# A four-block transformer layer for 16 sequences: which weights are prepared ahead of the step table

## The reference

```python
x = x + attn_a(layernorm(x), Wq, bq, Wk, bk, Wv, bv, Wo, bo)   # 16 heads, window of 32 either side, 4 global tokens, softmax
x = x + ffn(layernorm(x), w_gate, w_up, w_down)                # hidden 768, int32 weights / 127, silu(gate) * up
x = x + attn_b(layernorm(x), Wqkv, Wout, bout)                 # rotary, causal, denominator from scores without rotation
x = x + ffn(layernorm(x), w_gate, w_up, w_down)                # the same weights again
```

## Time and profile before

| | us |
|---|---|
| median of three runs | 2028.87 (2023.63 to 2030.54) |
| the profiled execution | 2020.54 |
| its span, first to last instruction | 2018.3 |
| TensorE busy | 1802.5 (89%) |
| VectorE busy | 1429.3 (71%) |
| ScalarE busy | 1429.0 (71%) |
| GpSimd busy | 803.8 (40%) |
| mean granted TensorE clock | 0.946 |

### The profile page before, as it was taken

The page is one execution under the profiler, slowest core; times in us unless marked ns, Lnnn a source line. Parts: engine busy times, 40 slices in busy tenths (PEclk is TensorE's granted clock), DMA queues, the critical chain, the costliest instruction groups (busy, mean ns, idle before and its releaser), DMA issues.

```text
span 2018.3 us, 63373 instructions
## 1 busy us (share of the span) xinstructions
PE 1802.5 (89%) x25221; PEld 1140.4 (57%) x25221; DVE 1429.3 (71%) x2978; ACT 1429.0 (71%) x3591; POOL 803.8 (40%) x1140
## 2 busy tenths in 40 slices
PE   5577999999899999999899999999999999998775
PEld 3363556566565655656565565656565565655444
DVE  6374768677686867768786877778786777865634
ACT  2227787786868778786877869686877868687590
POOL 0423343533434343443434344343435434344431
PEclk9687999999998999999999999999999999999897
DMA  5223344352524435253534525253443525243321
GB/s 155 64 56 90 87 129 98 100 119 77 136 63 131 91 101 124 78 130 69 137 78 116 122 76 127 72 134 70 138 100 89 127 75 139 61 125 90 73 68 36
DMA packets 129204, 199.51 MB, mean 99 GB/s; under 512 B 26720, under 2 KB 60512, under 8 KB 128880
## 3 DMA queue, kind: packets, MB, share of 16 engines
q1 hardware_dynamic: 128912, 195.44, 38.1%
HBM read 67.87 MB, written 51.52 MB: 59 GB/s over the span
## 4 chain that ended last, share of the span: by engine, by line
PE 47%; ACT 19%; DVE 16%; DMA 7%; issue 5%; SPq 3%; POOL 2%; POOLq 0%; DVEq 0%; ACTq 0%
PE psum L1120 14%; ACT psum L1236 7%; PE psum L1138 7%; ACT probs_B L1226 6%; PE psum L1150 5%; DMA xn<-o_scr_B 4%; PE psum L1017 4%; ACT probs_A L1219 3%; PE psum L1084 3%; PE psum L1094 3%; PE psum L1053 3%; DVE top L1410 2%; SPq L634 2%; PE psum L883 2%; PE psum L1038 2%
## 5 line engine op out<-in xcount | busy, mean ns | idle before, releaser
L1236 ACT ACTIVATE psum<-psum 128x512 f32<-128x512 f32 x1024 | 605.2, 598 | 164.4 <-PE psum L1017 163.5
L1659 POOL TENSOR_TENSOR h<-tmp,h 128x512 f16<-128x512 f32 x192 | 227.6, 1185 | 423.1 <-DVE h L1540 412.7
L1226 ACT ACTIVATE probs_B<-psum 128x512 f32<-128x512 f32 x640 | 334.5, 630 | 34.8 <-PE psum L1038 32.6
L1676 POOL TENSOR_SCALAR_AFFINE_SELECT probs_B<-probs_B 128x256 f32<-128x256 f32 x512 | 201.4, 421 | 117.7 <-ACT probs_B L1226 117.6
L1017 PE MATMUL psum<-pack_b 48*128 48x512 f16 x1024 | 176.9, 394 | 39.6 <-DMA pack_b<-src_b 20.3
L1120 PE MATMUL psum<-xT,w_u 128*128 128x256 f16 x1536 | 210.9, 278 | 1.2
L1120 PE MATMUL psum<-xT,w_g 128*128 128x256 f16 x1536 | 208.8, 280 | 3.1 <-ACT xT L1254 2.6
L1236 ACT ACTIVATION_READ_ACCUMULATOR psum<-psum 128x1 f32 x1024 | 204.2, 199 | 0.0
L1138 PE MATMUL psum<-w_d,h 128*128 128x256 bf16 x1536 | 194.7, 273 | 5.6 <-POOL h L1659 5.6
L1642 POOL TENSOR_TENSOR veps<-mv,eps 128x4 f32<-128x4 f32 x64 | 12.9, 202 | 426.0 <-DVE mv L1490 426.0
L1523 DVE SCALAR_TENSOR_TENSOR tmp<-tmp,psum 128x512 f32<-128x512 f32 x192 | 128.1, 680 | 69.9 <-ACT tmp L1265 69.3
(11 more groups left out here) (150 smaller groups left out, 3229.3 us busy)
## 6 DMA issues: line engine op xcount, KB each, us to landing
pack_b<-src_b SPq DMA_DIRECT2D x768, 64.0 KB, 2.4
pack_a<-src_a SPq DMA_DIRECT2D x384, 64.0 KB, 2.3
x<-in_L_attn_a_x_dram SPq DMA_DIRECT2D x32, 512.0 KB, 4.3
o_scr_A<-o_raw SPq DMA_DIRECT2D x64, 256.0 KB, 4.7
o_scr_B<-o_raw SPq DMA_DIRECT2D x64, 256.0 KB, 2.8
xn<-o_scr_A SPq DMA_DIRECT2D x32, 256.0 KB
rden_on<-r_scr_A SPq DMA_DIRECT2D x32, 256.0 KB
x_scr<-x SPq DMA_DIRECT2D x16, 512.0 KB, 3.1
```

Source lines behind the costliest of these rows:

```text
L1226: act.activation(probs["B"][:, i, :], score_bank("NP", n // 2, q, n % 2)[:, :], ACT.Exp, scale=SM_SCALE / W_SCALE ** 2)\
L1236: act.activation(bank[:, :], bank[:, :], ACT.Exp, scale=SM_SCALE / W_SCALE ** 2, accum_out=den[:, 0, j, 2 * tile + e, t:t + 1]).then_inc(d ...
L1659: pool.tensor_tensor(h[1][:, i % 2, :], tmp[:, i % 2, :], h[0][:, i % 2, :], ALU.subtract)\
L1676: ins = pool.affine_select(a, a, [[0, 2], [1, P]], ALU.is_ge, 0.0, base=0, channel_multiplier=-1)
```

## The change

Only the three banks of Wq, Wk and Wv are still prepared ahead of the table. All the rest becomes steps of a new block W0, which exist for sequence 0 alone: YO, YT and YS for Wo, WC for the casts, WM for the maxima, WT and WS for the transposes and the staging of the eleven FFN banks, WF and WP for the largest magnitude, WG for GpSimd's share, one instruction each, and YB for split_b. They take their banks from the same planner. On SP, Wq comes first, x behind Wk, and Wo, the FFN matrices, Wqkv and Wout behind all constants; the fills of pack_a no longer wait, because the casts now use the room of probs_B. TensorE walks the table up to the first G of sequence 0 outside of the two branches, and loads the flag there. All places of AT have new values; of those that existed before, only a selection stands here. Old lines of the engines' functions that are printed above are left out of the diff where new ones take their place.

```diff
@@ START, AT
-         for block in ("A", "PA", "VA", "NA", "OA", "F1", "PB", "VB", "RB", "B", "OB", "F2")}
+         for block in ("A", "PA", "VA", "NA", "OA", "F1", "PB", "VB", "RB", "B", "OB", "F2", "W0")}
...
-    "GM": (534.16,),
+    "GM": (533.22,),
-    "AT": (582.57, 625.43, 655.69, 677.7),
+    "AT": (581.33, 623.04, 659.31, 669.95),
-    "AO": (585.97, 626.12, 670.95, 678.73),
+    "AO": (579.62, 619.24, 663.37, 675.46),
-    "BO": (1266.42, 1343.16, 1397.14, 1471.83),
+    "BO": (1263.68, 1337.19, 1396.46, 1466.91),
-    "OBOL": (1450.55, 1472.59),
+    "OBOL": (1450.65, 1472.69),
...
+    "WC": (395.9, 422.98, 434.23),
+    "WM": (496.91, 497.15, 516.63),
+    "WT": (440.02, 440.08, 440.12, 440.22, 459.82, 460.12, 462.93, 473.27, 481.82, 485.41, 497.76),
+    "WS": (413.82, 431.49, 432.1, 432.2, 448.79, 449.91, 452.32, 453.04, 472.87, 473.35, 491.53),
+    "WP": (543.91,),
+    "WF": (542.43, 544.43),
+    "WG": (533.17, 533.27, 533.37, 558.07, 578.57, 598.07, 618.07, 638.07, 658.07),
+    "YB": (633.59,),
+    "YO": (400.12,),
+    "YT": (420,),
+    "YS": (436.01,),
...
+    for kind in ("WC", "WM", "WT", "WS", "WP", "WF", "WG", "YO", "YT", "YS", "YB"):
+        puts(kind, "W0")
...
+STEPS = sorted(((start_of(q, block) + place, kind, n, block, q) for q in range(SEQS) for place, kind, n, block in PLACES
+               if q == 0 or block != "W0"),
...
+        st_probs = probs["B"][:, :, :].rearrange("p a b -> p (a b)")
-        st_f32 = [stage(st_a, 0, FT * D), stage(st_a, FT * D, FT * D), stage(st_probs, 0, FT * D)]
-        st_ocols = stage(st_a, 2 * FT * D, KT, D)
+        st_f32 = [stage(st_probs, n * FT * D, FT * D) for n in range(3)]
+        st_ocols = stage(st_probs, 3 * FT * D, KT, D)
...
         def _(sp):
-            sp.dma_start(st_o, Wo.rearrange("(t p) n -> p t n", p=P)).then_inc(w_in[3], 16)
-            sp.dma_start(eye[:, :], eye_in).then_inc(eye_there, 16)
             for n, w in enumerate((Wq, Wk, Wv)):
                 sp.dma_start(st_qkv[n], w.rearrange("(t p) n -> p t n", p=P)).then_inc(w_in[n], 16)
-            for n, w in enumerate((w_gate, w_up, w_down)):
-                rows = w.shape[0] // P
-                dst = st_f32[n].bitcast(I32).rearrange("p (t n) -> p t n", t=rows)
-                sp.dma_start(dst, w.rearrange("(t p) n -> p t n", p=P)).then_inc(w_in[4 + n], 16)
-            sp.dma_start(x1[:, :, :], x_in[0].rearrange("(t p) n -> p t n", p=P)).then_inc(x1_new, 16)
+                if n == 0:
+                    sp.dma_start(eye[:, :], eye_in).then_inc(eye_there, 16)
+                elif n == 1:
+                    sp.dma_start(x1[:, :, :], x_in[0].rearrange("(t p) n -> p t n", p=P)).then_inc(x1_new, 16)
             for n, b in enumerate((bq, bk)):
                 sp.dma_start(qk_bias[:, 2 * n:2 * n + 2], b.rearrange("(t p) -> p t", p=P),
                              allow_slow_non_contiguous=True).then_inc(c_in, 16)
+            for dst, b in ((v_bias, bv), (o_bias[0], bo), (o_bias[1], bout)):
+                sp.dma_start(dst[:, :], b.partition_broadcast(P)).then_inc(c_in, 16)
             sp.dma_start(strip[:, :], strip_in).then_inc(c_in, 16)
             col = 0
             for m in (*band, eye_bf, glob_sel):
@@ -605,22 +625,23 @@
                 sp.dma_start(m[:, :], masks_in[:, col:col + n].bitcast(BF16)).then_inc(c_in, 16)
                 col += n
             sp.dma_start(sel[:, :], sel_in.bitcast(BF16)).then_inc(c_in, 16)
-            for dst, b in ((v_bias, bv), (o_bias[0], bo), (o_bias[1], bout)):
-                sp.dma_start(dst[:, :], b.partition_broadcast(P)).then_inc(c_in, 16)
             for dst, a in ((cos, cos_in), (sin, sin_in), (swap, swap_in)):
                 sp.dma_start(dst[:, :], a).then_inc(c_in, 16)
-
             sp.dma_start(v_scr.rearrange("a h d -> a (h d)"), v_fill_in).then_inc(fills_in, 16)
+            for e in range(2):
+                rows = pack_a[HB * e + ROWS:HB * e + HB, :, :, :, :].rearrange("p j q t s -> p j (q t s)")
+                sp.dma_start(rows, a_fill_in[e]).then_inc(fills_in, 16)
+            sp.dma_start(st_o, Wo.rearrange("(t p) n -> p t n", p=P)).then_inc(w_in[3], 16)
+            for n, w in enumerate((w_gate, w_up, w_down)):
+                rows = w.shape[0] // P
+                dst = st_f32[n].bitcast(I32).rearrange("p (t n) -> p t n", t=rows)
+                sp.dma_start(dst, w.rearrange("(t p) n -> p t n", p=P)).then_inc(w_in[4 + n], 16)
             sp.dma_start(st_bqkv, Wqkv.rearrange("(t p) n -> p t n", p=P)).then_inc(wb_in, 16)
             for jj in range(2):
                 for c2 in range(2):
                     rows = Wout.rearrange("(c u j r) n -> c j r u n", c=2, u=2, j=2)[c2, jj]
                     first = 4 * DH * jj + 2 * DH * c2
                     sp.dma_start(st_brows[first:first + 2 * DH], rows).then_inc(wb_in, 16)
-            sp.wait_ge(w_flag, 3)
-            for e in range(2):
-                rows = pack_a[HB * e + ROWS:HB * e + HB, :, :, :, :].rearrange("p j q t s -> p j (q t s)")
-                sp.dma_start(rows, a_fill_in[e]).then_inc(fills_in, 16)
...
@@ -788,38 +809,48 @@
         @block.tensor
         def _(pe):
+            pe.wait_ge(eye_there, 16)
+            for n in range(NQKV):
+                pe.wait_ge(w_in[n], 16)
                 for k in range(KT):
+                    for t in range(KT):
+                        last = pe.transpose(psum[n][:, k * D + t * P:k * D + (t + 1) * P], st_qkv[n][:, t, k * P:(k + 1) * P], eye[:, :])
+                last.then_inc(w_turned, 1)
+            pe.wait_ge(w_taken, NQKV)
+
+            def turn_o_weights():
+
+                bank_free("YT", 0, "W0", 0, 0)
+                bank = bank_of("YT", 0, "W0", 0)
+                pe.wait_ge(w_columns, 1)
+                for u in range(KT):
+                    for t in range(KT):
+                        last = pe.transpose(bank[:, u * D + t * P:u * D + (t + 1) * P], st_ocols[:, t, u * P:(u + 1) * P], eye[:, :])
+                last.then_inc(w_turned, 1)
+
+            def turn_ffn_weights(n):
+
+                bank_free("WT", n, "W0", 0, 0)
+                bank = bank_of("WT", n, "W0", 0)
+                if n < 8:
+                    w = st_f32[n // 4].rearrange("p (t n) -> p t n", t=FT)
+                    pe.wait_ge(w_f32, 1 + n // 4)
+                    k, half = n // 2 % 2, n % 2
+                    blocks = [(t * P, w[:, 3 * half + t, k * P:(k + 1) * P]) for t in range(3)]
                 else:
+                    w = st_f32[2].rearrange("p (t n) -> p t n", t=KT)
+                    pe.wait_ge(w_f32, 3)
+                    first = 2 * (n - 8)
+                    blocks = [(f * D + t * P, w[:, t, (first + f) * P:(first + f + 1) * P]) for f in range(2) for t in range(KT)]
+                for c0, a in blocks:
+                    last = pe.transpose(bank[:, c0:c0 + P], a, eye[:, :])
+                last.then_inc(w_shifted, 1)
+
+            def turn_top():
+
+                bank_free("WP", 0, "W0", 0, 0)
+                pe.wait_ge(w_spread, 1)
+                pe.transpose(bank_of("WP", 0, "W0", 0)[:, 0:P], w_row, eye[:, :]).then_inc(w_top_turned, 1)
             def bank_free(*key):
...
+            split = min(i for i, step in enumerate(STEPS) if step[1] == "G")
+
+            def program(steps, exact):
...
@@ -1194,10 +1239,13 @@
                     elif kind == "W":
                         swap_step(n, q)
+            program(STEPS[:split], True)
+            pe.wait_ge(w_flag, 3)
+            is_general = pe.value_load(general[0:1, 0:1], min_val=0, max_val=1)
             with pe.If(is_general < 1):
-                program(True)
+                program(STEPS[split:], True)
             with pe.Else():
-                program(False)
+                program(STEPS[split:], False)
 
         @block.scalar
...
+            def stage_weights(n):
+
+                act.wait_ge(w_shifted, n + 1)
+                bank = bank_of("WT", n, "W0", 0)
+                if n < 8:
+                    k, half = n // 2 % 2, n % 2
+                    dst = [a[:, k, half * 3 * P:(half + 1) * 3 * P] for a in ((w_g, w_u)[n // 4][0], (st_gT, st_uT)[n // 4])]
                     given = bank[:, 0:3 * P]
                 else:
+                    f = 2 * (n - 8)
+                    if n == 8:
+                        act.wait_ge(w_taken, NQKV)
+                    dst, given = [a[:, f:f + 2, :] for a in (w_d[0], st_dT)], bank[:, :].rearrange("p (k n) -> p k n", k=2)
                 act.activation(dst[0], given, ACT.Copy)
                 act.activation(dst[1], given, ACT.Copy).then_inc(w_staged, 1)
+
             for _, kind, n, block, q in STEPS:
+                if kind == "WS":
+                    stage_weights(n)
+                elif kind == "A2E":
                     a_exponential(2 * n, q)
                     a_exponential(2 * n + 1, q)
...
@@ -1343,50 +1397,48 @@
                 high = parts[0].bitcast(F32) if scale < 1 else parts[0]
```

(70 more changed lines are left out.)

301 lines of the change are left out of this document (118 added, 183 removed), and 66 rows, old and new, of the table AT.

## The result

| | before | after |
|---|---|---|
| median in the same group of runs, us | 2026.34 (2023.63 to 2030.54, 4 executions) | 2002.28 (1999.55 to 2262.77, 4 executions) |
| profiled execution, us | 2020.54 | 2003.88 |
| its span, us | 2018.3 | 2002.1 |
| TensorE busy, us | 1802.5 | 1771.9 |
| mean granted clock in the profile | 0.946 | 0.959 |

One execution of the changed kernel took 2262.77 us, at a mean granted clock of 0.736 against 0.957 to 0.959 in the others, and the ratio leaves it out; the median of the other three is 2000.68. The ratio is 0.988 [0.9859, 0.9902]: some 24 us less, where -10.8 was forecast and the range ended at 2004. The change is faster by about 1.2%, more than twice what the sum said.

What follows compares the result with a forecast made beforehand. TensorE was taken to bound 15 turns of 115.0 us, leaving only the start to gain. Terms -14.8 + 0.5 + 2.0 + 0 + 0.5 + 1.0 + 0 = -10.8 us gave a median of 2018.1, range 2004 to 2030.

Steps and rivals of the forecast that it cites:

- Part 1: Start: first normalisation (bn_stats) begins near 11.0 us instead of 25.8, a gain of 14.8 us, bounds 13.7 and 16.
- Part 2: Start, sequence 0: x_low may wait for the constants to land and biases to be scaled; cost 0 to 1.5, taken +0.5.
- Part 3: Attention's first phase, sequence 0: 44 moved transposes and their staging cost 0 to 4 us, taken +2; VectorE's share 0.
- Part 4: GpSimd's nine steps, before L1 of sequence 1: cost 0, with 3.7 us of cover.
- Part 5: Value phase: split_b on VectorE between AT1 and AT2 delays AT2; cost 0 to 1.2, taken +0.5.
- Part 6: Value load and If on TensorE before sequence 0's first G, no longer hidden; cost 0 to 5.54, taken +1.0.
- Part 7: New order of steps in the turns: bounds -0.5 and +0.5 us a turn, taken as 0.
- a better turn: Rival: half a us less idle time in each of 14 turns, another -7, giving 2011; chance 0.10.
- The sign that I had set: Prediction fails if the turn differs from 115.0 by 0.5 us or more, or the first normalisation starts after 14.
- Swallowed: Rival: first-turn costs give back 12.2 of the 14.8 us, giving 2026.3; chance 0.20 together with late constants.
- constants late: Rival: constants still arrive when they did, x_low at 22.6, net -6.5, 2022.4; chance 0.20 together with the swallowed gain.
- The slower one: Rival: attention B's output load waits behind attention A's store on SP in 14 turns; 2034.9 at 1.2 us each; chance 0.11.

Runs made afterwards that it cites:

- split_b experiment: Changed kernel with split_b (YB) moved to place 401, ahead of the maxima of sequence 0: 2006.42 us, ratio 0.9914 to the kernel before.
- three sequences: Both kernels computing only sequences 0 to 2, thirteen left out: 508.38 us before, 494.11 us changed, difference -14.3.
- the two half-changed kernels: Changed kernel's new steps at the old places: 2017.68 us, ratio 0.9957; kernel before with its old steps at the new places: 2020.0 us, ratio 0.996.
- the repeated change: Changed kernel, unaltered, timed again beside the kernel before: 2004.21 us, ratio 0.9888.

## Why the prediction was wrong, point by point

**Part 1 was right.** Wv's transposes began at 8.39 (forecast 8.4), bn_stats at 10.88 (forecast 11.0): -14.9 us for -14.8. Over five profiles of before and seven of the changed kind it starts at 25.1 and 10.7 on average, -14.4.

**Part 2** (+0.5) cost nothing. The biases were scaled by 16.4 us, 1.3 ahead of x_low, and x_low came 6.8 us behind bn_stats, as before. The bound 0 was the right end. The pack loads were free to start at 26.59, as said.

**Part 3** (+2.0) cost 1.2 in this pair (14.9 at bn_stats, 13.7 at ntopT) and 0.5 over the same twelve profiles (14.4 and 13.9). Even of that, part lies outside of the phase and is no cost of the change: ahead of it the 24 projection matmuls took 7.33 us where they took 6.34 before, because nine instead of four ran at over 600 ns instead of 379; but they took 7.51 in the second profile of before, and 6.0 to 7.5 in all. The granted clock of the phase was not the half one of the earlier trace rows for long. The same window of the changed kernel, and two of the phase in which the transposes and their staging stand (busy PE, PEld, DVE, ACT, POOL; granted clock; DMA share; GB/s):

```profile
46.00:76.00 30.00, 17.81 (x648) 12.30 (x653) 22.98 (x28) 14.86 (x29) 24.34 (x10) 0.83 0.14 43
38.00:42.25 4.25, 4.25 (x53) 3.26 (x47) 2.85 (x6) 3.01 (x8) 0.00 (x0) 0.51 0.60 104
42.25:50.40 8.15, 5.93 (x109) 4.20 (x101) 7.54 (x15) 6.38 (x15) 0.72 (x1) 1.00 0.16 38
```

At 46 to 76 us it is 2.4 GHz for more than half of the time. In the staging phase it is still half (0.51) from 38.00 to 42.25, where the moved transposes keep TensorE busy without a gap, and 1.00 from 42.25 on, with TensorE busy 5.93 of 8.15 us. On that point the trace sides with the sentence cited from the Trainium skill, TensorE: Matmul & The Clock Gate, Part 1, "activity releases the throttle". I had written that TensorE would be nearly full and still charged the middle of the range. (That it was busy under half of the old window was misread: 15.14 of 30 us in the earlier trace rows is half, and only 5.61 of 12.43 in the earlier trace rows is less.) VectorE, put at 0, is busy for 7.54 of these 8.15 us and is the tightest engine there.

**Part 4** (0) held on the path: L1 of sequence 1 still finds GpSimd idle for 6.00 us, where it had 3.74.

```profile
80.38 0.20 POOL L1708 TENSOR_TENSOR veps<-mv,eps 128x4 f32<-128x4 f32 x1 [6.00 <-DVE mv L1542]
```

But its cover was named wrongly. The cost of GpSimd's steps is not on GpSimd: they hold up VectorE instructions, as the rows of the split_b experiment show.

**Part 5** (+0.5): where it stands, about 3 us were lost (AT1 came 14.8 us sooner than before, bn_stats of sequence 1 only 11.8), and nothing of it is left at the first store. But split_b is not what lost them, since moving it away won 0.4; the two holes in TensorE between its sums with the values, 1.27 and 3.96 us where they were 0.80 and 1.65, account for most of it, and the prediction had no term for them. WP, said to be what A2-1 waits for if the ntopT rows came sooner, became exactly that. Timelines of TensorE, VectorE and GpSimd:

```profile
57.87 0.45 PE L853 MATMUL psum<-eye,x 128*128 128x128 f32 x1 [4.37 <-DVE x L1430]
58.24 0.64 PE L920 MATMUL psum<-band,eye_bf 64*64 64x512 bf16 x4
...
49.77 5.07 DVE L1423 TENSOR_REDUCE x<-probs_B 128x1 f32<-128x1536 f32 x3
...
55.06 2.66 DVE L1430 COPY x<-x 128x128 f32<-128x128 f32 x1
...
54.55 3.09 POOL L1771 TENSOR_TENSOR w_g<-src_b,w_g 128x1536 bf16<-128x1536 f32 x1
```

The copy's row in the kernel before, where GpSimd is idle:

```profile
22.68 0.23 DVE L1381 COPY rden_on<-newton 128x128 f32<-128x128 f32 x1
```

TensorE waits 4.37 us there for VectorE, whose three maxima (5.1 us) and a copy of 2.66 us stand ahead; 2.4 of the 2.66 are a hold by GpSimd's instruction, which ends at 57.64, like the copy at 57.72. For the path this is little: A2-1 comes 7.8 us behind ntopT (58.24 - 50.44) where it came 7.1 before (71.25 - 64.18), so WP costs it 0.7. The first store still comes 14.0 us earlier on average, so none of that is lost there.

**Part 6** (+1.0) was 0: no hole, and no gain without the branch.

So the start's net is -14.3 (three sequences), where the sum had -10.8. Small costs of 0.5, 2.0, 0.5 and 1.0 were charged, and 3.5 of the 4.0 did not come: a third of what the sum was off by.

**Part 7 is the step that failed**: "I see no row that says which way; bounds -0.5 and +0.5 us a turn; 0". The turn became shorter by about 0.5 (116.6 to 116.2 by the medians, uncertain by 0.2), the lower bound, and thirteen to fourteen turns make 6 to 7 us of it. This is the rival "a better turn" in size, not in mechanism: I had it as idle time won back, and TensorE's idle time in a turn grew from 7.0 to 8.3 us while its busy time fell from 109.5 to 107.9. Less time at the half clock, 6.4 to 4.0 us a turn, is what the rows show in its place, and the new places cause it; that it is what shortens the turn is not shown, because the two half-changed kernels do not bear it out. The cause of these 6 to 7 us stays open. -14.3 and -6.5 make -20.8. The ratios say -22.7 for the repeated change and -24 for the first executions; those last 2 to 3 us are within their intervals (0.9917 would be -17) and no row claims them. One step before that was wrong in itself. I read the turn as 115.0 from the mean over 15 stores, which mixes in two short ones at the ends (107.9 and 107.1); inner turns average 116.5, of which the earlier trace rows happened to show one of the shorter. The sign that I had set, a turn off 115.0 by 0.5 us, could not show the failure either: by the same reading the changed kernel's turn is (1871.5 - 144.7)/15 = 115.1.

**The rivals.** "Swallowed" and "constants late" fell with parts 2, 3 and 6. The slower one did not come about: in a middle turn the second load of OB goes and VectorE waits for it 2.74 us, where it was 3.57.

```profile
963.77 0.68 DVE L1493 TENSOR_TENSOR o_raw<-o_raw,psum 128x512 f32<-128x512 f32 x1
...
966.07 0.65 SPq L750 DMA_DIRECT2D xn<-o_scr_B  x1
...
970.76 0.69 DVE L1506 TENSOR_TENSOR xn<-xn,rden_on 128x512 f32<-128x512 f32 x1 [2.74 <-DMA xn<-o_scr_B]
```

AT1 ends at 964.45, 1.6 us ahead of that load, so AO1 had not become the later of the two.

## What to carry to other kernels

A new order of steps that repeats in every turn needs a term of its own even where no instruction is added and no idle time is in sight: half a microsecond in each of thirteen turns was a third of this gain. Read the turns one by one with their granted clock before taking a mean, but do not take less time at the half clock for less time: here one half-changed kernel had the first and hardly the second. Where the effect is spread over the run, run both kernels at two or three lengths; the shortest gives the start, the difference gives the turn. And when several small costs each rest on a bound that nothing in the trace approaches, their middles add up to a cost that isn't there.
